# In the slot of a group's mean, feed-forward products ahead of the mean on TensorE, and the centring behind the gated products on VectorE

## The reference, cut to what matters

```
x = attn_layer(shift_tokens(x), Wqkv[i], q_scale[i], k_scale[i], Wo[i]) + x
x = ffn_layer(shift_tokens(x), ln_g[i], ln_b[i], W1[i], b1[i], W2[i], b2[i]) + x

def ffn_layer(x, g, bln, W1, b1, W2, b2):
    mu = x.mean(-1, keepdims=True)
    var = ((x - mu) ** 2).mean(-1, keepdims=True)
    xn = (x - mu) / jnp.sqrt(var + 1e-05) * g + bln
    a, gate = jnp.split(xn @ W1 + b1, 2, -1)
    return a * jax.nn.gelu(gate, approximate=False) @ W2 + b2
```

## Time and profile before

| | us |
|---|---|
| median of three runs | 3917.49 |
| lowest and highest run | 3913.91, 3923.57 |
| profiled execution, its own time | 3918.71 |
| span of the profiled execution | 3916.9 |
| outside the span (3918.71 - 3916.9) | 1.8 |
| PE busy (share of the span) | 3581.4 (91%) |
| DVE busy | 3162.1 (81%) |
| ACT busy | 2652.5 (68%) |
| POOL busy | 2432.0 (62%) |

### The profile page before, as it was taken

One profiled execution on the slowest core, in us unless ns is written; L12 is line 12 of the kernel. 1 busy time (PEld: TensorE's weight loads), 2 busy tenths in 40 slices (PEclk: granted clock), 3 DMA queues, 4 the chain that ended last, 5 costly groups with the idle time before them and its releaser, 6 DMA issues.

```text
span 3916.9 us, 146395 instructions
## 1 busy us (share of the span) xinstructions
PE 3581.4 (91%) x60128; PEld 2226.2 (57%) x60128; DVE 3162.1 (81%) x4377; ACT 2652.5 (68%) x4972; POOL 2432.0 (62%) x2197
## 2 busy tenths in 40 slices
PE   5676776899999999999999999999999999999997
PEld 2222222566666666666666666666666666666664
DVE  4899998888878778888878788778787887888884
ACT  3555554677777777767776777677777777676765
POOL 0355554876666666666666666666666666666661
PEclk9889898999999999999999999999999999999999
DMA  3000000111111111111110111111111111110101
GB/s 76 0 0 0 0 0 0 34 32 31 31 42 41 34 30 31 31 47 38 35 32 26 42 42 36 32 31 31 45 37 33 31 31 47 36 36 27 32 28 37
DMA packets 64418, 120.05 MB, mean 31 GB/s; under 512 B 18196, under 2 KB 35986, under 8 KB 63634
## 3 DMA queue, kind: packets, MB, share of 16 engines
q1 hardware_dynamic: 63762, 110.70, 9.7%
HBM read 20.50 MB, written 2.10 MB: 6 GB/s over the span
## 4 chain that ended last, share of the span: by engine, by line
PE 53%; DVE 15%; issue 9%; ACT 7%; POOL 0%; ACTq 0%; DMA 0%; DVEq 0%; POOLq 0%; SPq 0%
PE ob L1187 10%; PE qk L1129 9%; PE sc L1214 7%; PE trb L1001 6%; PE vob L1195 4%; PE vob L1135 4%; PE sc L1163 4%; DVE arena L888 3%; PE sc L1221 3%; DVE ssq L894 3%; DVE mx L901 3%; PE ob L1001 2%; DVE arena L889 2%; ACT arena L619 2%; DVE xnT L978 1%
## 5 line engine op out<-in xcount | busy, mean ns | idle before, releaser
L507 POOL TENSOR_TENSOR arena<-arena,rnorm 128x512 f32<-128x512 f32 x768 | 793.7, 1054 | 929.3 <-ACT rnorm L626 928.8
L500 POOL TENSOR_TENSOR arena<-arena 128x512 f32<-128x512 f32 x768 | 961.7, 1274 | 84.9 <-DVE arena L889 84.9
L633 ACT ACTIVATE arena<-trb 128x512 f32<-128x512 f32 x768 | 465.7, 606 | 432.4 <-PE trb L1001 432.4
L1129 PE MATMUL qk<-wqkv,xs 128*128 128x512 f32 x1536 | 734.2, 601 | 16.0 <-issue 8.9
L888 DVE TENSOR_TENSOR arena<-qk,tab_q 128x512 f32<-128x512 f32 x384 | 263.7, 687 | 504.6 <-ACT arena L619 499.6
L483 POOL TENSOR_TENSOR arena<-arena 128x512 f32<-128x512 f32 x256 | 299.9, 1180 | 345.4 <-DVE arena L858 329.9
L1001 PE MATMUL trb<-ident,arena 128*128 128x128 f32 x3072 | 483.0, 280 | 10.7 <-ACT arena L633 7.6
L619 ACT ACTIVATE arena<-qk 128x512 f32<-128x512 f32 x768 | 433.5, 592 | 79.4 <-PE qk L1129 65.5
L1129 PEld LDWEIGHTS qk<-wqkv,xs 128*128 128x128 f32 x1536 | 294.5, 193 | 312.0 <-issue 294.8
L894 DVE TENSOR_REDUCE ssq<-arena 128x16 f32<-128x1024 f32 x384 | 464.3, 1209 | 0.0
L514 POOL TENSOR_TENSOR arena<-arena,rinv 128x512 f32<-128x512 f32 x384 | 392.4, 1043 | 65.8 <-DVE rinv L911 65.8
(11 more groups left out here) (139 smaller groups left out, 6020.5 us busy)
## 6 DMA issues: line engine op xcount, KB each, us to landing
arena<-arena SPq DMA_DIRECT2D x192, 384.0 KB, 3.2
arena<-arena SPq DMA_DIRECT2D x192, 64.0 KB, 3.0
wqkv<-in_L_ffn_Wqkv SPq DMA_DIRECT2D x18, 512.0 KB, 4.3
wo<-in_L_ffn_Wo SPq DMA_DIRECT2D x6, 512.0 KB, 4.0
arena<-in_L_attn_x SPq DMA_DIRECT2D x8, 256.0 KB, 2.8
out<-arena SPq DMA_DIRECT2D x8, 256.0 KB, 2.2
w<-in_L_ffn_W SPq DMA_DIRECT2D x6, 341.0 KB, 2.9
arena<-in_sel SPq DMA_DIRECT2D x1, 1024.0 KB, 5.0
```

Source lines behind the costliest of these rows:

```text
L500: nc.gpsimd.tensor_tensor(ts[c * 2 + j][:, heads], tu[:, 0, heads], tu[:, 1, heads], ALU.add).then_inc(summed[0], 1)
L507: nc.gpsimd.tensor_tensor(part, part, rnorm[j][:, 8 * h:8 * h + 8].unsqueeze(2).to_broadcast([P, 8, HEAD]), ALU.mult) \
L633: A((qT, kT)[j][u][:, 4 * h:4 * h + 4, at_col:at_col + P], TRB.rearrange("p (a t) -> p a t", a=4), ACT.Copy) \
L1129: MM(QK[:, 512 * h:512 * h + 512], lhsT=xs[u][:, c * P:(c + 1) * P], rhs=wqkv[:, col:col + 512], start=True, stop=True) \
```

## The change

On TensorE the mean's product is issued after the products with W1 of the same slot instead of before the variance. On VectorE the centring is issued after the calls of `hidden` instead of before them. No instruction, wait or semaphore is added or removed. The mean keeps its two waits (`ln_in` and `x_added`), and takes them along.

```
 DVE, layer_slot:
+                at_ = group_at(l, k, LAG_UP[1])
+                if at_:
+                    hidden(*at_, 0, 3, 512)
+                at_ = group_at(l, k, LAG_UP[2])
+                if at_:
+                    hidden(*at_, 1, 4, 0)
+                    hidden(*at_, 2, 5, 512)
                 at_ = group_at(l, k, LAG_MEAN)
                 if at_:
                     item(dve, ln_mean, at_[1] + 2 * GROUPS)
                     V.tensor_tensor(xc[0], xs2.rearrange("p s t -> p (s t)"), bank[2][:], ALU.subtract).then_inc(ln_xc[0], 1)
-                at_ = group_at(l, k, LAG_UP[1])
-                if at_:
-                    hidden(*at_, 0, 3, 512)
-                at_ = group_at(l, k, LAG_UP[2])
-                if at_:
-                    hidden(*at_, 1, 4, 0)
-                    hidden(*at_, 2, 5, 512)
 PE, layer_slot:
                 mean = group_at(l, k, LAG_MEAN)
-                if mean:
-                    pe.wait_ge(ln_in[0], mean[1] + 1)
-                    if out_before:
-                        item(pe, x_added, out_before[0])
-                    MM(VOB[:, :], lhsT=meanw[:], rhs=xs2.rearrange("p s t -> p (s t)"), start=True, stop=True).then_inc(ln_mean[0], 1)
                 var = group_at(l, k, LAG_VAR)
                 ...
                         up(*at_, parts, scored)
+                if mean:
+                    pe.wait_ge(ln_in[0], mean[1] + 1)
+                    if out_before:
+                        item(pe, x_added, out_before[0])
+                    MM(VOB[:, :], lhsT=meanw[:], rhs=xs2.rearrange("p s t -> p (s t)"), start=True, stop=True).then_inc(ln_mean[0], 1)
```

More of the change, by code:

```diff
@@ L951, in layer_slot @@
                     maxima(*at_)
-                at_ = group_at(l, k, LAG_MEAN)
-                if at_:
-                    item(dve, ln_mean, at_[1] + 2 * GROUPS)
-                    V.tensor_tensor(xc[0], xs2.rearrange("p s t -> p (s t)"), bank[2][:], ALU.subtract).then_inc(ln_xc[0], 1)
                 at_ = group_at(l, k, LAG_UP[1])
@@ L962, in layer_slot @@
                     hidden(*at_, 2, 5, 512)
+                at_ = group_at(l, k, LAG_MEAN)
+                if at_:
+                    item(dve, ln_mean, at_[1] + 2 * GROUPS)
+                    V.tensor_tensor(xc[0], xs2.rearrange("p s t -> p (s t)"), bank[2][:], ALU.subtract).then_inc(ln_xc[0], 1)
                 at_ = group_at(l, k, LAG_DOWN)
```

## The result

The changed kernel is slower: 3965.24 us median of four runs (3957.47 to 3978.01) against 3916.15 (3913.91 to 3923.57); ratio 1.0125, 95% interval 1.0092 to 1.0159. Forecast were 3933 us and a range of 3922 to 3950. The direction was right, the size was not: 49 us instead of 15.

The account below looks back on a forecast made before the run. The prediction took TensorE to bound the kernel, stalled before the mean by a full VectorE. 45 slots 3 longer by 0.34 us (15.3), less 0.6 in the tail, gave 14.7 us slower: 3933 us, range 3922 to 3950.

Parts of the forecast that it names:

- The view to begin with: TensorE's one dear wait is before the mean in 45 slots 3, 1.27 us each, because VectorE is full.
- the first rule weighed: Keep the matmul engine busy (change worth 62 us); where it idles, improve the engines blocking it (change worth nothing).
- What goes: In slot 3 the stall before the mean, 1.50 us, goes; TensorE is 1.37 us ahead at the turns.
- What comes: In slot 3 `v_unit` waits for the later centring; each of 45 slots grows by 0.34 us.
- What is late next: In slots 4 and 5 ScalarE is 1.06 us late, VectorE 0.80; idle time covers it, TensorE loses nothing more.
- Rival 2: Lateness of ScalarE and VectorE in slot 4 reaches TensorE: up to 48 us slower, 3966 us; chance 0.11, whole or part.
- The tail: After the steady stretch, products go ahead of one mean that waits 0.61 us: 0.6 us gained.
- The sum: Whole kernel: 45 x 0.34 = 15.3 us, less 0.6, gives 14.7 us slower, 3933 us.

Follow-up runs that it names:

- TensorE's half alone: The kernel before with only TensorE's order changed (products with W1 first, the mean behind them): 3888.51 us, ratio 0.9911.
- VectorE's half alone: The kernel before with only VectorE's order changed (centring behind the calls of `hidden`): 3935.69 us, ratio 1.0029.
- the kernel with the longest stop: The kernel before with an added VectorE reduction of 1152 columns ahead of the addition to x in slot 3: 4026.84 us, ratio 1.0263.

## Why the prediction was wrong

The view to begin with named the right wait, and it came back elsewhere. But "VectorE is full whatever TensorE does first" does not mean that TensorE has to wait. With TensorE's half alone VectorE is busy for 8.32 of the slot's 8.64 us, and TensorE's longest stop is 0.20 us instead of 1.26. The wait came back because the change put the centring behind the gated products. The second half of the first rule weighed (by which a new order is worth nothing, since it takes no work from VectorE) fails by the same run: an order alone gained 0.9%.

**What goes** was right. The products with W1 start at 1.72 us into the slot, the mean at 3.44 without a wait. The turns start at 4.30, where I had put 4.43.

**What comes** was right but for the restart. I took 0.34 us a slot; it is 0.28. The centring ended 8.94 us into the slot as computed (1927.91 - 1918.97). But `v_unit` followed 0.05 us after it (median of the 45), not 0.15, and took 0.96 to the next unit, not 0.93. The 0.15 was read from the end of the addition to the start of the mean, and does not carry over to this pair. Where the clock stays up, the change costs 12.6 us by this sum, and the kernel with VectorE's half alone, as long in slot 3, is 10.1 us slower than the kernel before on its chip.

**What is late next** was right. The rotation of slot 4 starts at 12.42 us (forecast 12.45), after 2.14 us of idle time (2.2). In the changed kernel the addition in slot 4 and the variance of slot 5 follow so:
```profile
2372.35 0.42 DVE L918 TENSOR_TENSOR xT<-vob,xT 128x256 f32<-128x256 f32 x1
...
2373.46 1.02 PE L1237 MATMUL vob<-arena,meanw 128*128 128x512 f32 x2
...
2377.10 0.75 DVE L930 SCALAR_TENSOR_TENSOR xT<-sc,lpar,xT 128x512 f32<-128x512 f32 x1 [0.49 <-PE sc L1221]
```
The addition ends 0.69 us before the variance, which does not wait, and 0.49 of the 0.89 us of idle time are left before line 930. Rival 2 came within 1 us of the measured time by its number (3966 against 3965.24). That is luck: it would have been the wrong reason, as TensorE has no new wait in slots 4 to 6.

**The tail** gained 0.6 us, as forecast: from the last unit to the end of the span 94.3 us instead of 94.9.

**The sum** is the step that failed. It has no term for TensorE's clock. (3933.4 less 1.2 is 3932, not 3933; this changes nothing.) I priced a stop as its length and took two stops of nearly the same length as equal. The profiled slot showed a clock of 1.00 with a stop of 1.26 us in it, and I took that for a property of stops of this size. The missing term is 28 x 1.70 = 47.6 us in the profiled execution. The trace before had a hint that I did not follow up. It has 5 falls in the steady stretch. Three stand at the ends of loop bodies, where TensorE stops for over 2 us. The other two stand in a slot 7, at an issue stop amid the products of line 1187 that is shorter than the 1.26 us before the mean:
```profile
2229.20 0.42 PE L1187 MATMUL ob<-arena 64*64 64x32 f32 x11 [1.12 <-issue]
...
2230.04 1.86 PE L1135 MATMUL vob<-wqkv,xs 128*128 128x512 f32 x2
```
The product of line 1135 takes 1.86 us here, and 1.02 at full clock. One more issue stop of 1.12 us, at 1695.8, brought no fall. So already before the change a stop of 1.12 us at one place twice brought a fall that none of 45 stops of 1.26 us at another did.

The experiments show each part of this. Filled, the stop costs no fall; moved back before the mean, it costs none, even at 1.72 us; before `v_unit` the falls grow with its length; before the mean it takes a longer stop to bring them. The Trainium skill (TensorE: Matmul & The Clock Gate, A second HAM failure mode: psum-queue depth-cycling) tells of a kernel in which short idle times between groups of matmuls make the clock swing between its two levels, and puts the cost between the bursts. The trace agrees on the swing. The cost it shows is in the products themselves that run at 1.2 GHz: four records in 3.24 us instead of 1.88, and a busy time of TensorE that grew by 51.2 us.

Two things stay open. Why the place matters: before `v_unit` the stop follows the small products of line 1187 and the turns, before the mean it follows the output product and the unit's products. The falls of the kernel before in slot 7 come at stops with small products on both sides. No run separates what stands before the stop from what stands behind it. And why a stop of the same 1.51 us brings a fall in one group and none in another: falls come in successive groups and then stay away for several, and differ between executions. In such a series the fall begins later in the slot from group to group (8.99, 9.31, 9.64 and 9.74 us in the groups at 2825 to 3029 us of the changed kernel), so the moment of a stop seems to count as well. That was not tried.

The origin of the issue stops was not tried either, but the traces point to one. All 212 issue stops in the lists of small products, in the steady stretches of the eleven traces, end 1.2 to 1.7 us after the end of a transfer of the profile's kind "instruction" (queue q8). Of a sample of the products of line 1187 (every 37th), 5 to 10% start at such a distance from one. That points to the loading of instructions; no run changes it.

## What to carry to other kernels

Ask two questions of a stop that is to be moved: through which wait each half of the change acts (TensorE's order alone gave 0.9%, VectorE's centring ahead of the rotation on top of it 1.0% together, and the centring behind `hidden` cost 0.3% without any fall), and what TensorE's clock does at the new place. Here a rise of TensorE's busy time with the same products was the mark of a lower clock; look at the granted clock by stage before looking for a new wait. An engine that is busy for 97% of a slot need not be what bounds it: try the order first. Judge the halves of a change one by one: here one half was worth -0.9%, the other +0.3%, and together they gave +1.2%.

## What the runs showed of the hardware

- The granted clock fell from 2.4 to 1.2 GHz for 3.41 us at a time, and a fall at slot 3 cost 1.70 us in the median of the changed kernel (1.48 to 1.70 in the kernel with the longest stop). Every fall in the steady stretches of the eleven traces began during a stop of TensorE of over 0.7 us or at most 2.1 us after its end. Stops before `v_unit` of 0.86, 1.12, 1.50 and 1.52 us brought 0, 2, 28 and 21 falls in 45; stops before the mean of 1.26, 1.72 and 2.52 us brought 0, 0 and 25.
- The scatter of a kernel goes with its mean granted clock: 20.5 us over four runs of the changed kernel at 0.968 to 0.973, 16.2 us over 19 runs of the kernel before at 0.975 to 0.982, and 2.0 us over ten of VectorE's half alone at 0.979 to 0.981.
- When TensorE's waits in slot 3 went away, stops called issue amid the lists of 128 small products grew from 5.1 us to 22.2. Those 17 us are nearly all of the 18 that were missing from the 62 forecast.
